# A graph network on one core: where the last bias enters PSUM, and how gathered rows are turned

## The reference

```python
def sage(x, src, dst, Wl, bl, Wr):
    summed = segment_sum(x[src], dst, N)
    mean = summed / maximum(segment_sum(1, dst, N), 1)
    return mean @ Wl.T + bl + x @ Wr.T
h = relu(sage(x, ..., Wl0, bl0, Wr0))
h = relu(sage(h, ..., Wl1, bl1, Wr1))
x1 = layernorm(x + sage(h, ..., Wl2, bl2, Wr2))
# second layer: edge attention (q, k, v from nodes and edges, softmax over src), then
out = layernorm(x1 + (v_nodes - agg) @ W_out)
```

## Time and profile before

| | |
|---|---|
| median of 3 runs | 2645.54 us (2643.79 to 2648.65) |
| profiled execution, its own time | 2644.61 us |
| its span, first to last instruction | 2642.8 us |
| PE busy, share of the span | 1873.9 us, 71% |
| POOL | 1770.9 us, 67% |
| DVE | 1729.4 us, 65% |
| ACT | 1095.2 us, 41% |
| mean granted PE clock | 0.854 of full speed |

### The profile page before, as it was taken

The page is one execution under the profiler, slowest core; times in us unless marked ns, Lnnn a source line. Parts: engine busy times, 40 slices in busy tenths (PEclk is TensorE's granted clock), DMA queues, the critical chain, the costliest instruction groups (busy, mean ns, idle before and its releaser), DMA issues.

```text
span 2642.8 us, 43434 instructions
## 1 busy us (share of the span) xinstructions
PE 1873.9 (71%) x10441; PEld 1316.8 (50%) x10441; DVE 1729.4 (65%) x5671; ACT 1095.2 (41%) x2508; POOL 1770.9 (67%) x1895
## 2 busy tenths in 40 slices
PE   4755666999989999677777673888788877770000
PEld 2324565666656666455555453555555555540000
DVE  7787886777767777565555533888888878881000
ACT  7951111544534444122222222777666666650000
POOL 0046776566756676467777777777777777766776
PEclk7558999999999999788888885999999999995555
DMA  0025666788877887545445623455445445433321
GB/s 19 1 56 148 165 159 138 174 195 189 177 172 187 189 192 173 154 125 135 126 128 142 164 68 106 144 158 157 144 143 152 145 140 152 140 104 104 94 92 51
DMA packets 366730, 357.03 MB, mean 135 GB/s; under 512 B 46534, under 2 KB 288724, under 8 KB 366584
## 3 DMA queue, kind: packets, MB, share of 16 engines
q1 hardware_dynamic: 310136, 246.40, 31.0%
q0 software_dynamic: 56448, 109.10, 20.3%
HBM read 232.83 MB, written 129.11 MB: 137 GB/s over the span
## 4 chain that ended last, share of the span: by engine, by line
PE 32%; POOL 26%; issue 17%; DVE 13%; DMA 5%; ACT 5%; POOLq 1%; DVEq 0%; SPq 0%; ACTq 0%
POOL GX L675 10%; POOL hsrc L675 9%; PE bank L852 9%; PE bank L872 5%; POOL out_dram L729 4%; PE bank L774 3%; PE bank L900 3%; PE bank L892 3%; PE bank L890 3%; DMA GX<-in_x_dram,idx_a 3%; PE bank L856 2%; ACT normed L1021 2%; ACT normed L1022 2%; DVE stats L1358 2%; POOL x_prime L729 2%
## 5 line engine op out<-in xcount | busy, mean ns | idle before, releaser
L675 POOL DMA_INDIRECT GX<-mean_product,idx_a x392 | 411.2, 1049 | 129.5 <-issue 113.9
L675 POOL DMA_INDIRECT GX<-in_x_dram,idx_a x392 | 378.1, 965 | 117.9 <-issue 108.9
L852 PE MATMUL bank<-h,wt 128*128 128x512 f32 x588 | 321.0, 657 | 0.1
L1046 ACT ACTIVATE logv<-mv,eps 128x4 f32<-128x4 f32 x245 | 72.2, 295 | 541.5 <-DVE mv L1363 541.4
L729 POOL DMA_INDIRECT x_prime<-normed,idx_b x196 | 197.6, 1008 | 88.0 <-issue 83.4
L729 POOL DMA_INDIRECT out_dram<-XN,idx_b x196 | 192.8, 984 | 76.0 <-issue 64.8
L675 POOL DMA_INDIRECT hsrc<-x_prime,idx_d x196 | 189.7, 968 | 59.7 <-issue 59.7
L675 POOL DMA_INDIRECT GX<-in_edge_attr_dram,idx_a x196 | 189.7, 968 | 58.6 <-issue 53.5
L675 POOL DMA_INDIRECT hsrc<-x_prime,idx_c x196 | 186.7, 953 | 59.7 <-issue 59.7
L774 PE MATMUL bank<-ident,GX 128*128 128x128 f32 x588 | 104.5, 307 | 155.5 <-DMA GX<-in_x_dram,idx_a 149.5
L774 PE MATMUL bank<-ident,hsrc 128*128 128x128 f32 x468 | 86.5, 316 | 119.0 <-DMA hsrc<-x_prime,idx_d 57.4
(11 more groups left out here) (231 smaller groups left out, 4656.0 us busy)
## 6 DMA issues: line engine op xcount, KB each, us to landing
mean_product<-prod SPq DMA_DIRECT2D x147, 256.0 KB, 4.3
hsrc<-mean_product SPq DMA_DIRECT2D x147, 256.0 KB, 4.4
XN<-in_x_dram SPq DMA_DIRECT2D x98, 256.0 KB, 4.5
x_prime<-normed SPq DMA_DIRECT2D x98, 256.0 KB
XN<-x_prime SPq DMA_DIRECT2D x98, 256.0 KB, 4.5
out_dram<-normed SPq DMA_DIRECT2D x98, 256.0 KB
flag<-same_dst_row SPq DMA_DIRECT2D x147, 128.0 KB, 4.3
XN<-low_row SPq DMA_DIRECT2D x98, 128.0 KB
```

The costliest lines, as they stand in the source:

```text
L675: pool.indirect_dma_start(buf[:, c.slot(U), t, :], None, table, bass.IndirectOffsetOnAxis(ap=idx[:, c.slot(U), t:t + 1], axis=0)).then_inc ...
L852: last = pe.matmul(psum[:, :], wt[:, T_R[i], :], before[:, c.slot(2), :], start=True, stop=not dst_phase)
```

## The change

1. The bias of y. The bias row is loaded onto all 128 partitions. `chain_y` loses its opening product (L870); in its place ACT writes the bias, repeated four times, into y's bank with a Copy from SBUF (`bias_y`), and the four products of h2 add to it. `bias_y` waits for DVE to have added x to the chunk that used the bank before; `chain_y` waits for `bias_y`. ACT's order gains `(8, bias_y)` at its end in mean1 and mean2 and `(3, bias_y)` at its end in dst. The set-up on DVE that split the bias into three bf16 parts goes, and ones3 with it.
2. Two products on PE with the identity, 128x512 in float32, write banks 6 and 7 once between mean0 and mean1, ahead of the first `bias_y` (`y_cleared`).
3. `mean_turn` turns the gathered rows with PE's transpose in all three mean stages, and in mean1 and mean2 the product of node rows comes behind them and adds to them.

```diff
--- before.py
+++ after.py
@@ -206,12 +206,7 @@
         wexp_rows = sb("wexp_rows", [P, H])
         wexp_rep = sb("wexp_rep", [P, H, HD])
         bcol = sb("bcol", [P, 2])
-        b2 = sb("b2", [3, D])
-        b2part = sb("b2part", [3, 3, D], BF16)
-        b2rest = sb("b2rest", [3, 2, D])
-        b2mask = sb("b2mask", [3, 3, D], BF16)
-        b2row = sb("b2row", [3, TPC, D], BF16)
-        ones3 = sb("ones3", [3, P], BF16)
+        b2 = sb("b2", [P, D])
 
         hsrc = sb("hsrc", [P, EP])
         carved = [0]
@@ -370,6 +365,7 @@
         zero_out = sem("zero_out")
         pad_ready = sem("pad_ready")
         all_out = sem("all_out")
+        y_cleared = sem("y_cleared")
 
         signals = []
 
@@ -404,6 +400,7 @@
         u1_done, u1_kept = signal("u1_done", 2, 1, CHAIN), signal("u1_kept", 2, 1, CHAIN)
         u2_done, u2_kept = signal("u2_done", 2, 1, CHAIN), signal("u2_kept", 2, 1, CHAIN)
         y_done = signal("y_done", 2, 1, NORM)
+        y_biased = signal("y_biased", 2, 1, CHAIN)
         added0 = signal("added0", 2, 1, DST)
         added = signal("added", 2, 1, CHAIN)
         n_stats, n_aggr = signal("n_stats", 2, 1, NORM), signal("n_aggr", 2, 1, NORM)
@@ -518,7 +515,7 @@
                 sp.dma_start(wexp_rows[HD * h:HD * (h + 1), :], Wexp[h:h + 1, :].to_broadcast([HD, H])).then_inc(small_loaded, 16)
             for i, b in enumerate((bl0, bl1)):
                 sp.dma_start(bcol[:, i:i + 1], b.rearrange("(p a) -> p a", a=1)).then_inc(small_loaded, 16)
-            sp.dma_start(b2[:, :], bl2.rearrange("(a n) -> a n", a=1).to_broadcast([3, D])).then_inc(small_loaded, 16)
+            sp.dma_start(b2[:, :], bl2.rearrange("(a n) -> a n", a=1).to_broadcast([P, D])).then_inc(small_loaded, 16)
 
             for i in range(2):
                 sp.dma_start(prod_table[i][EP:EP + P, :], zrow[:, :]).then_inc(zero_out, 16)
@@ -867,10 +864,10 @@
                 pe.wait_ge(u2_kept.of(c), u2_kept.after(c))
                 pe.wait_ge(added.of(c), added.free(c))
                 y = bank[6 + c.slot(2)]
-                pe.matmul(y[:, :], ones3[:, :], b2row[:, :, :].rearrange("k t d -> k (t d)"), start=True, stop=False)
+                pe.wait_ge(y_biased.of(c), y_biased.after(c))
                 for t in range(TPC):
                     last = pe.matmul(y[:, t * P:(t + 1) * P], h2[:, c.slot(2), t * P:(t + 1) * P], wt[:, T_R[2], :],
-                                     start=False, stop=t == TPC - 1)
+                                     start=False, stop=t == TPC - 1, skip_group_check=True)
                 last.then_inc(y_done.of(c), 1)
 
             def mean_turn(c):
@@ -882,15 +879,12 @@
                 else:
                     pe.wait_ge(m_h.of(c), m_h.after(c, 1))
                     psum = bank[5]
-                if c.phase == "mean0":
-                    for t in range(TPC):
-                        last = turn_in(psum[:, t * P:(t + 1) * P], GX[:, c.slot(U), t, 0:D])
-                else:
+                for t in range(TPC):
+                    last = pe.matmul(psum[:, t * P:(t + 1) * P], GX[:, c.slot(U), t, 0:D], ident[:, :], is_transpose=True,
+                                     start=t == 0, stop=c.phase == "mean0" and t == TPC - 1)
+                if c.phase != "mean0":
                     i = int(c.phase[-1]) - 1
-                    pe.matmul(psum[:, :], wt[:, T_R[i], :], take_cols(hsrc, c.index() * CH, CH), start=True, stop=False)
-                    for t in range(TPC):
-                        last = pe.matmul(psum[:, t * P:(t + 1) * P], GX[:, c.slot(U), t, 0:D], ident[:, :],
-                                         start=False, stop=t == TPC - 1)
+                    last = pe.matmul(psum[:, :], wt[:, T_R[i], :], take_cols(hsrc, c.index() * CH, CH), start=False, stop=True)
                 last.then_inc(m_turned.of(c), 1)
 
             def mean_prod(c):
@@ -933,6 +927,8 @@
                 if i == 0:
                     run(pe, "mean0", [(LAG + 1, mean_turn), (0, look_up), (LAG, mean_prod)], NC, middle=table_sums)
                     look_done.end(pe, "mean0")
+                    for one in (6, 7):
+                        pe.matmul(bank[one][:, :], ident[:, :], hsrc[:, 0:CH], start=True, stop=True).then_inc(y_cleared, 1)
                 else:
                     dense = first if i == 1 else second
                     run(pe, f"mean{i}", [(1, mean_prod), (3, mean_turn), (DENSE + 4, dense(chain_t)), (DENSE + 3, dense(chain_1)),
@@ -1038,6 +1034,11 @@
                 act.wait_ge(u2_done.of(c), u2_done.after(c))
                 act.wait_ge(y_done.of(c), y_done.free(c))
                 act.activation(h2[:, c.slot(2), :], bank[2][:, :], ACT.Relu, bias=bcol[:, 1:2]).then_inc(u2_kept.of(c), 1)
+
+            def bias_y(c):
+                act.wait_ge(added.of(c), added.free(c))
+                act.activation(by_tile(bank[6 + c.slot(2)][:, :]), b2[:, :].rearrange("p (a d) -> p a d", a=1).to_broadcast([P, TPC, D]),
+                               ACT.Copy).then_inc(y_biased.of(c), 1)
 
             def inverse_root(c):
 
@@ -1065,11 +1066,13 @@
                     m_seg.end(act, f"mean{i - 1}")
                 if i == 0:
                     run(act, "mean0", [(0, mean_keep)], NC)
+                    act.wait_ge(y_cleared, 2)
+                    act.wait_ge(small_loaded, 16 * (H + 3))
                 else:
                     dense = first if i == 1 else second
                     run(act, f"mean{i}", [(3, mean_keep), (DENSE + 4, dense(keep_t)), (DENSE + 3, dense(keep_1)),
-                                          (DENSE + 2, dense(keep_2)), (DENSE + 1, dense(inverse_root))], NC)
-            run(act, "dst", [(4, keep_t), (3, keep_1), (2, keep_2), (1, inverse_root)], NC)
+                                          (DENSE + 2, dense(keep_2)), (DENSE + 1, dense(inverse_root)), (DENSE + 3, dense(bias_y))], NC)
+            run(act, "dst", [(4, keep_t), (3, keep_1), (2, keep_2), (1, inverse_root), (3, bias_y)], NC)
             y_done.end(act, "dst")
 
 
@@ -1158,7 +1161,6 @@
 
             dve.memset(kin[:, :, :], N).then_inc(pad_ready, 1)
             dve.memset(zrow[:, :], 0.0).then_inc(pad_ready, 1)
-            link(dve.memset(ones3[:, :], 1.0))
             link(dve.memset(eps[:, :], EPS))
             link(dve.memset(carry_row[:, :, :], 0.0))
             link(dve.memset(seg[:, :, :], 0.0))
@@ -1294,19 +1296,6 @@
             link(dve.tensor_scalar(wexp_rep[:, :, :], wexp_rows[:, :].rearrange("p (h a) -> p h a", a=1).to_broadcast([P, H, HD]),
                                    float(HD) ** -0.5, None, ALU.mult))
 
-            link(dve.tensor_copy(b2part[:, 0, :], b2[:, :]))
-            link(dve.tensor_tensor(b2rest[:, 0, :], b2[:, :], b2part[:, 0, :], ALU.subtract))
-            link(dve.tensor_copy(b2part[:, 1, :], b2rest[:, 0, :]))
-            link(dve.tensor_tensor(b2rest[:, 1, :], b2rest[:, 0, :], b2part[:, 1, :], ALU.subtract))
-            link(dve.tensor_copy(b2part[:, 2, :], b2rest[:, 1, :]))
-            for i in range(3):
-                link(dve.tensor_scalar(b2mask[:, i, :], b2part[:, i, :], ident[0:3, i:i + 1], None, ALU.mult))
-            link(dve.tensor_tensor(b2mask[:, 0, :], b2mask[:, 0, :], b2mask[:, 1, :], ALU.add))
-            link(dve.tensor_tensor(b2mask[:, 0, :], b2mask[:, 0, :], b2mask[:, 2, :], ALU.add))
-            for t in range(TPC):
-                link(dve.tensor_copy(b2row[:, t, :], b2mask[:, 0, :]))
-
-
             dve.wait_ge(near_in, 64)
             link(dve.tensor_tensor(same[:, :], keyf[:, 0, :], near[:, 0, 0, :], ALU.is_equal))
             link(dve.tensor_tensor(resetf[:, :], keyf[:, 1, :], near[:, 1, 0, :], ALU.not_equal))
```

## The result

The changed kernel takes 2637.29 us (median of 6 runs, 2634.17 to 2643.03), the kernel before 2645.9 in the same comparison (2641.6 to 2648.65): a ratio of 0.9971 [0.996, 0.9982]. The profiled execution of the changed kernel took 2643.03 us (span 2641.2).

What follows compares the result with a forecast made beforehand. PE bounds mean1 and mean2 at 6.21 us a step, afterwards the DVE-ACT circle at 5.90. Set-up -3.5 and 82 steps x 0.30 = -24.6 sum to -28.1 from 2644.6; forecast median 2617 us, range 2606 to 2637.

Steps and rivals of the forecast that it cites:

- Set-up: DVE's bias-splitting instructions before the first stage go, so what follows moves up: -3.5 us, bounds 0 and 3.7.
- Clearing products: Two PE products between mean0 and mean1, 3.4 us, covered by PE's 4.90 us idle gap: 0, bounds 0 and +0.9.
- PE's savings: In each mean1 and mean2 step, L870 gone saves 0.31 us, transposes for identity passes 0.46: 6.21 to 5.44.
- D: Rival: transposes cost what the eight passes did, PE's step 5.90; time as forecast, sharing its 0.76 chance.
- The price of the bias copy: How long bias_y holds ACT in each step: 0.52 us, bounds 0.50 and 0.69.
- B: Rival: bias_y is dear, at 1.0 us costing more than PE gives: 2657 us, chance 0.07.
- The circle: DVE-ACT chain from one add of x to the next in mean1 and mean2: 5.38 us, 5.90 with bias_y.
- A: Rival: the circle gives way, hiding 0.50 us, and POOL bounds at about 5.6: 2593 us, chance 0.11.
- POOL, 5.58, next in line: Four gathers with gaps take POOL 5.58 us a step, hidden behind 5.90 and the next bound.
- The clock: PE's granted clock in mean1 once PE idles; estimated 0.95 at 92% busy, making its step 5.73, still hidden.
- C: Rival: PE's clock falls to 0.88, its step is 6.2 again, only set-up gains: 2642 us, chance 0.06.
- Dst: POOL's gathers and puts fill the dst stage, PE and ACT have slack: 0, bounds -0.3 and +0.5 us.

Runs made afterwards that it cites:

- e1: The changed kernel, loading only one of four row tiles of x in the looped steps of mean1 and mean2; 2609.52 us, ratio 0.986.
- e2: The changed kernel with bias_y placed ahead of the root in ACT's order in mean1, mean2 and dst; 2640.73 us, ratio 0.9989.
- e4: The changed kernel with the old mean_turn (eight identity passes behind the product of node rows); 2636.96 us, ratio 0.9968.
- f1: The changed kernel with gathered zero rows spread over the table's 128 zero rows instead of always row EP; 2612.15 us, ratio 0.9856.
- f2: e2 with the gathered zero rows spread over 128 rows instead of always row EP; 2572.79 us, ratio 0.9704.
- f4: e2 with e1's lighter load of x, zero rows not spread; 2639.04 us, ratio 0.9959.
- g2: The changed kernel with the old mean_turn and the gathered zero rows spread over 128 rows; 2610.34 us, ratio 0.9853.
- g4: f1 with the gathered zeros spread over 8 rows instead of 128; 2611.81 us, ratio 0.9854.
- e3: The kernel before with the new mean_turn alone, the bias staying on PE and its set-up on DVE; 2640.63 us, ratio 0.998.
- f3: The kernel before with the gathered zero rows spread over 128 rows; 2650.06 us, ratio 0.9999.
- g1: The kernel before with the new mean_turn alone and the gathered zero rows spread over 128 rows; 2608.07 us, ratio 0.9844.
- g3: The kernel before with every row gathered in mean1 and mean2 taken from row EP; 2897.81 us, ratio 1.0936.

## Why the forecast fell short

- *Set-up, -3.5 forecast.* POOL resumes at 220.78 (224.70 in the earlier trace rows), 3.9 us earlier, but the first add of mean1 comes 2.3 us earlier (452.74 for 455.08). One profile is a poor measure of that, however. In the nine profiles with the new bias (after, e1, e2, e4, f1, f2, f4, g2, g4) that first add comes at 449.28 to 454.90, mean 453.0, in the four without it (before, e3, f3, g1; g3, with its slower gathers, is left aside) at 455.08 to 459.83, mean 457.5. So the term is about -4.5; it was forecast a little small.

```profile
220.78 0.19 POOL L662 COPY idx_a<-col_i 128x16 int32 x1 [3.65 <-PE bank L883]
```

- *Clearing products, 0 forecast.* They start while PE waits for x, hold it to 442.01, and no wait follows (against the earlier trace rows). Right.

```profile
438.95 2.72 PE L931 MATMUL bank<-hsrc,ident 128*128 128x512 f32 x4 [1.86 <-DVE lookup L1445]
442.01 1.09 PE L771 MATMUL bank<-ident,XN 128*128 128x128 f32 x4 [0.34 <-issue]
```

- *PE's savings, 0.31 and 0.46.* Four transposes take 0.43 us (581.75 to 582.18), 0.49 where PE had just waited (825.37 to 825.86), so 0.46 is right, and D is out. The 0.31 was too small. Without L870 its neighbours are shorter as well: in g2's rows the two layers hold PE 1.72 (1.82 in the earlier trace rows) and y 0.89 (1.00), so the bias product cost 0.52. PE's step with both halves is thus about 5.23, not 5.44. It changes nothing in the forecast, since the circle is longer.
- *The price of the bias copy, 0.52.* Measured 0.52. B is out. (By the Trainium skill, ScalarE: Activation LUTs, What ACT_TABLE_LOAD costs, the prediction had come to the same estimate, and the trace agrees: 824.12 to 824.64.)
- *The circle, 5.90.* Measured 5.84 over the undisturbed steps of the changed kernel and 5.83 over the 82 full steps of f1, inside 5.80 to 6.17. Without the copy it was put at 5.38, and e2's undisturbed steps and f2 average 5.4. (The 5.10 that the prediction ascribes to rows 4 is from rows 5.) A is out: taking the copy off the circle makes the undisturbed steps shorter, and f2 shows what that is worth. (The Trainium skill, PSUM: Partial Sum Buffer, Engine vs sequencer instructions, says that ScalarE's queue is strictly first in, first out. The trace agrees: the copy gets into ACT's idle stretch only where program order puts it there, at 820.13 in e2 and at 824.12, behind the root, in the changed kernel.)
- *POOL, 5.58, next in line.* This is no lower bound: f2's steps average 5.42. The mean gather took POOL 1067 ns in the earlier trace rows and takes 1040 in f2.
- *The clock.* 0.97 in mean1 with its stalls, 1.00 in f1, where PE is busy for 235.11 of 254 us and the prediction had estimated 0.95 for about that share. C is out.
- *Dst, 0.* POOL 348.87 of 460 us, with 0.30 of issue between its instructions. Right as far as one pair of profiles tells.
- *The step that failed* is the sentence "The DMA share was 0.85 at 6.20, which becomes 0.89", and with it "So the new step is the largest of PE 5.44, POOL and the circle 5.90", in which the transfers have no term. The share was read as a load that grows with the rate and is hidden as long as it is below 1. It was 0.92 with stalls, and 0.96 in the stretch 500 to 560 us, where the backlog grows, at 187 GB/s; f2 moves 209 GB/s at 0.76. What it missed is that the engines' time went to reads of one row, whose packets grow longer under load: a gather packet took 633 ns in the kernel before, 774 in the changed one and 845 in f4. At 6.20 us a step loads land after 4.6 us; at 5.84 the backlog grows to 18 and 25 us and the engines stand still. That was put at nothing, and it cost 31 us.

The sum with the terms as measured between the two profiled executions is -2.3 for the first stage, 82 x (6.20 - 5.84) = -29.5, and +31 of stalls, so -0.8, where the span falls by 1.6. The forecast's 28.1 and the measured 8.6 are compared by medians. The profiled execution of the changed kernel was its slowest run; the median is 5.7 below it. Without the row (f1) the change is worth 39.2 us against the kernel before on its chip, 8.6 with it, so the row takes 31. For the change itself 28.1 was thus too small: by the circle (82 x 0.06 = 4.9), the first stage (1.0), and what was put at 0 (as far as the pair f3 and f1 tells, 0.7 at the ends of the phases, 1.1 between them and 2.5 behind them). The nearness of 2637.29 to the range's upper end is luck: two errors, 31 us of stalls left out and 11 us of gain left out, partly cancel.

What stays open: what in the memory makes reads of one row slow, why the backlog begins to grow at just 500 us and not before, and how the slow transfers delay SP's issues (5.11 us for one) in detail.

## What to carry to other kernels

When a change shortens the step of a full engine, ask of every hidden resource what its share is made of, not only how large it is: here queue q0 had 40.5% for 10.35 MB beside 44.1% for 36.28 MB, and that pair of lines, on record before the change, was the hint. Then look at how long loads take to land, step by step: a time that grows is a backlog, even while no engine waits. If a gather has a default row (padding, zeros, missing keys), give it several copies and spread the indices; it cost nothing measurable here (f3) and turned 8.6 us of gain into 39.2, and with the bias copy moved into 78.6. And put new work on an engine into the stretch in which it idles, since program order decides, not the average load.

## What was unexpected of the hardware

Many reads of one 512-byte row are slow here. A gather packet of 4096 bytes (8 rows), on average over 480 to 720 us, took 234 ns in the kernel before with the row spread, 633 with 65% of the rows at one address, 1469 with all of them; in the changed kernel 295, 774 and, at the shorter step of f4, 845. The kernel before with all rows at one address needs 397.6 and 405.7 us from the first to the last add of mean1 and mean2, which is 25,088 row reads each, so about 16 ns for a read (an estimate, other work of the DMA engines included). With 65% there, some 16,300 reads, that is an estimated 260 us. It is no sharp bound: e1 runs its phases in 273 us without a stall, the changed kernel, which moves more besides, would have 272 (f1) and takes 15 to 17 us more, and e2 and f4, whose steps would allow 253, take 283 to 291. The DMA share does not tell how much more could be moved: it was 0.95 at 134 GB/s in g3 and 0.76 at 209 GB/s in f2.
